# Last FFN of a fused attention and FFN layer: the fourth token group of the batch before it goes behind the transposes of its input, with rounded passes ahead of remainders

## What is computed

```python
def _L0_ffn_ref(x, ln_gamma, ln_beta, fc1_q, fc1_scales, fc1_bias, fc2_q, fc2_scales, fc2_bias):
    ...
    h = (x - mu) * jax.lax.rsqrt(var + EPS) * ln_gamma + ln_beta
    hf = h.reshape(-1, H)
    w1 = _dequant(fc1_q, fc1_scales, G)
    y = hf @ w1 + fc1_bias
    y = jax.nn.silu(y)
    w2 = _dequant(fc2_q, fc2_scales, G)
    z = y @ w2 + fc2_bias
    return residual + 0.5 * z.reshape(residual.shape)
x = L0_attn_x
x = x + _L0_attn_ref(_layernorm(x, axis=-1), L0_attn_Wq, L0_attn_bq, L0_attn_Wk, ...)
x = x + _L0_ffn_ref(_layernorm(x, axis=-1), L0_ffn_ln_gamma, L0_ffn_ln_beta, ...)
```

## Time and profile before

| | us |
|---|---|
| median of 3 runs | 1546.86 |
| lowest, highest | 1544.33, 1548.13 |
| profiled execution, its time | 1547.17 |
| profiled execution, its span | 1545.3 |

### The profile page before, as it was taken

The page is one execution under the profiler, slowest core; times in us unless marked ns, Lnnn a source line. Parts: engine busy times, 40 slices in busy tenths (PEclk is TensorE's granted clock), DMA queues, the critical chain, the costliest instruction groups (busy, mean ns, idle before and its releaser), DMA issues.

```text
span 1545.3 us, 40671 instructions
## 1 busy us (share of the span) xinstructions
PE 1500.6 (97%) x14820; PEld 1307.8 (85%) x14820; DVE 1285.4 (83%) x2587; ACT 1131.0 (73%) x1917; POOL 671.1 (43%) x466
## 2 busy tenths in 40 slices
PE   5799999999999999999999999999999999999997
PEld 5588888888888888888888888888888888888887
DVE  6888888888888888888888888888888888888865
ACT  4487777787777787777787777787777787777763
POOL 3245344544344544344544344544344444344443
PEclk8899999999999999999999999999999999999999
DMA  7946775555775555775556775556775556765540
GB/s 197 218 104 130 176 175 134 138 126 133 176 176 124 140 131 135 176 176 123 123 145 138 176 163 139 132 130 141 176 166 129 127 138 146 176 173 124 112 97 28
DMA packets 153944, 222.96 MB, mean 144 GB/s; under 512 B 20032, under 2 KB 71488, under 8 KB 153920
## 3 DMA queue, kind: packets, MB, share of 16 engines
q1 hardware_dynamic: 152560, 222.63, 60.6%
q10 hardware_dynamic: 1360, 0.01, 0.1%
HBM read 138.69 MB, written 83.89 MB: 144 GB/s over the span
## 4 chain that ended last, share of the span: by engine, by line
PE 89%; DVE 6%; issue 3%; DMA 1%; ACT 0%; SPq 0%; DVEq 0%; POOL 0%; ACTq 0%
PE ring L328 35%; PE ring L390 7%; PE ring L391 7%; PE num L496 6%; PE sc L454 6%; PE sc L328 5%; PE num L463 3%; PE num L328 3%; PE state_acc L328 3%; PE ring L528 2%; PE state_acc L477 2%; PE state_acc L454 1%; DVE xt_lo L654 1%; DVE qk L743 1%; DVE probs L624 1%
## 5 line engine op out<-in xcount | busy, mean ns | idle before, releaser
L1028 POOL TENSOR_TENSOR s_lo<-silu_f,s_hi 128x512 fp32r<-128x512 f32 x256 | 342.9, 1345 | 498.3 <-ACT s_hi L900 498.2
L624 DVE TENSOR_TENSOR probs<-sc,causal 128x512 f32<-128x512 f32 x416 | 271.5, 685 | 71.8 <-PE sc L454 62.0
L328 PE MATMUL ring<-w_hi,s_hi 128*128 128x256 f32 x992 | 282.7, 285 | 1.8 <-issue 1.8
L328 PE MATMUL ring<-w_lo,s_hi 128*128 128x256 f32 x992 | 279.4, 282 | 0.0
L328 PE MATMUL ring<-w_hi,s_lo 128*128 128x256 f32 x992 | 279.3, 282 | 0.0
L328 PEld LDWEIGHTS ring<-w_hi,s_hi 128*128 128x128 f32 x992 | 187.9, 189 | 15.7 <-issue 14.4
L1044 POOL TENSOR_TENSOR qk<-qk,phi_q 128x512 f32<-128x512 f32 x64 | 82.9, 1296 | 262.6 <-DVE qk L677 262.6
L328 PEld LDWEIGHTS ring<-w_lo,s_hi 128*128 128x128 f32 x992 | 188.2, 190 | 1.3
L328 PEld LDWEIGHTS ring<-w_hi,s_lo 128*128 128x128 f32 x992 | 188.0, 190 | 0.0
L390 PE MATMUL ring<-gt_hi,w_q 128*128 128x512 f32 x441 | 187.4, 425 | 0.0
L889 ACT ACTIVATE silu_f<-ring,bias,scale 128x512 f32<-128x512 f32 x217 | 167.4, 771 | 14.1 <-PE ring L391 11.5
(11 more groups left out here) (189 smaller groups left out, 3816.2 us busy)
## 6 DMA issues: line engine op xcount, KB each, us to landing
k_stack<-k_rows SPq DMA_DIRECT2D x192, 256.0 KB, 4.0
q_stack<-q_rows SPq DMA_DIRECT2D x384, 128.0 KB, 6.3
k_rows<-silu_f SPq DMA_DIRECT2D x128, 256.0 KB, 3.8
q_rows<-probs SPq DMA_DIRECT2D x128, 256.0 KB, 4.1
x_in<-in_x SPq DMA_DIRECT2D x32, 512.0 KB, 8.6
xb<-in_x SPq DMA_DIRECT2D x32, 512.0 KB, 8.3
out<-clip SPq DMA_DIRECT2D x64, 256.0 KB, 7.8
silu_f<-in_q SPq DMA_DIRECT2D x2, 512.0 KB, 10.7
```

The source lines that it names most:

```text
L328: last = e.matmul(target, a, b, start=(n == 0), stop=(n == 3 * len(pairs) - 1))
L624: masked[r].done(e.tensor_tensor(half_probs(u, r), score_bank(u, r)[:, :].rearrange("p (h q) -> p h q", h=HV), causal[:, None, :].to_broad ...
L1028: sl.done(e.tensor_tensor(s_lo[:, j, :], silu_f[:, j % SLOTS, :], s_hi[:, j, :].bitcast(F32), ALU.subtract))
```

## The change

Six edits, all of which bear on passes 31 and 32 only (`not A` means pass 32, `not N` passes 31 and 32):

1. The last token group of batch 30, fc2(3), is made in pass 32, behind the transposes of ffn_in and ahead of fc1(0), and its final(1) stands in pass 32 behind gt_lo on DVE.
2. fc2 without N waits for s_hi and s_lo of one feature group at a time.
3. fc2_group makes its eight products with s_hi first and waits for s_lo only ahead of the last four.
4. fc1 waits for gt_lo by half, and TAIL's first pair is swapped, so that the first product of fc1(0) goes to num1.
5. The residual of batch 31 is made behind ffn_sum(2) and no longer ahead of the first ffn_scaled.
6. POOL adds the bias to it by token group, two behind remainder 4 and two behind remainder 5.

```diff
-        TAIL = ((num[0], num[1]), (state_acc, ring[0]), (ring[1], ring[2]))
+        TAIL = ((num[1], num[0]), (state_acc, ring[0]), (ring[1], ring[2]))
...
-                w.need(ht_l, -1)
                 cols = slice(j * P, (j + 1) * P)
                 for t in range(T):
-                    if A or j == 0:
+                    w.need(ht_l, -1, t)
+                    if not A and j == 0:
+                        w.need(attn, -1, 1)
+                    elif A:
                         free_bank(w, f"f{j}{'ab'[t]}", present)
...
-            def fc2(c):
+            def fc2(c, shift=-1):
 
                 if not Fn:
                     return
-                w.need(sh, -1)
-                w.need(sl, -1)
                 n, h = divmod(c, 2)
                 if h == 0:
                     free_bank(w, f"z{n}", present)
+
+                def slices(j):
+                    w.need(sh, shift, j if not N else FT - 1)
+                    w.need(sl, shift, j if not N else FT - 1)
+
                 toks = slice(c * P, (c + 1) * P)
                 last = pe_split3(e, ring_bank(f"z{n}")[:, h * D:(h + 1) * D], [
-                    ((s_hi[:, j, toks], s_lo[:, j, toks]), (w2_hi[:, j, :], w2_lo[:, j, :])) for j in range(FT)])
+                    ((s_hi[:, j, toks], s_lo[:, j, toks]), (w2_hi[:, j, :], w2_lo[:, j, :])) for j in range(FT)], slices)
...
             def fc2_group(j):
 
                 w.need(sh, -1, j)
-                w.need(sl, -1, j)
...
                 for c in range(C):
-                    n, h = divmod(c, 2)
                     toks = slice(c * P, (c + 1) * P)
-                    z = z_bank(n, A)[:, h * D:(h + 1) * D]
-                    e.matmul(z, s_hi[:, j, toks], w2_hi[:, j, :], start=(j == 0 and h == 0), stop=False,
+                    e.matmul(target(c), s_hi[:, j, toks], w2_hi[:, j, :], start=(j == 0 and c % 2 == 0), stop=False,
                              skip_group_check=True)
-                    e.matmul(z, s_hi[:, j, toks], w2_lo[:, j, :], start=False, stop=False, skip_group_check=True)
-                    last = e.matmul(z, s_lo[:, j, toks], w2_hi[:, j, :], start=False, stop=(j == FT - 1),
-                                    skip_group_check=True)
-                    if j == FT - 1 and h:
+                    e.matmul(target(c), s_hi[:, j, toks], w2_lo[:, j, :], start=False, stop=False, skip_group_check=True)
+                w.need(sl, -1, j)
+                for c in range(C):
+                    last = e.matmul(target(c), s_lo[:, j, c * P:(c + 1) * P], w2_hi[:, j, :], start=False,
+                                    stop=(j == FT - 1), skip_group_check=True)
+                    if j == FT - 1 and c % 2:
                         z_pe.done(last)
...
+            if not A:
+                fc2(3, -2)
             fc1(0)
             fc1(1)
...
-            fc2(3)
+            if N:
+                fc2(3)
...
             if Fn and not A:
-                residual()
+                final(1, -2, z_bank(1, True))
...
             ffn_sum(2)
+            if not A and Fn:
+                residual()
...
-            if Fn:
+            if Fn and (N or not A):
                 final(1)
...
                 ffn_lo(j)
-            if Fn:
+                if Fn and not A and j in (4, 5):
+                    w.need(res_m, -1)
+                    for c in (2 * j - 8, 2 * j - 7):
+                        last = e.tensor_tensor(res[:, c, :], res[:, c, :], bias_2[:, :], ALU.add)
+                    if j == 5:
+                        e_res.done(last)
+            if Fn and A:
                 w.need(res_m, -1)
                 e_res.done(e.tensor_tensor(res[:, :, :], res[:, :, :], bias_2[:, None, :].to_broadcast([P, C, D]), ALU.add))
```

More of the change, by code:

```diff
@@ L414, in fc2_group, with target @@
                         w.need(masked[r], -1)
+                def target(c):
+                    return z_bank(c // 2, A)[:, c % 2 * D:(c % 2 + 1) * D]
                 for c in range(C):
-                    n, h = divmod(c, 2)
                     toks = slice(c * P, (c + 1) * P)
-                    z = z_bank(n, A)[:, h * D:(h + 1) * D]
-                    e.matmul(z, s_hi[:, j, toks], w2_hi[:, j, :], start=(j == 0 and h == 0), stop=False,
+                    e.matmul(target(c), s_hi[:, j, toks], w2_hi[:, j, :], start=(j == 0 and c % 2 == 0), stop=False,
                              skip_group_check=True)
-                    e.matmul(z, s_hi[:, j, toks], w2_lo[:, j, :], start=False, stop=False, skip_group_check=True)
-                    last = e.matmul(z, s_lo[:, j, toks], w2_hi[:, j, :], start=False, stop=(j == FT - 1),
-                                    skip_group_check=True)
-                    if j == FT - 1 and h:
+                    e.matmul(target(c), s_hi[:, j, toks], w2_lo[:, j, :], start=False, stop=False, skip_group_check=True)
[4 more added lines that the diff above has]
+                    if j == FT - 1 and c % 2:
                         z_pe.done(last)
@@ L743, in attention, with final @@
                 attn.done(e.tensor_tensor(qk[:, t, :], num[t][:, :], qk[:, t, :], ALU.mult))
[L745 to L749, removed]
+            def final(n, shift=-1, bank_=None):
+                w.need(z_pe, shift, n)
+                w.need(e_res, shift)
+                w.need(store, shift - 1)
                 cs = slice(2 * n, 2 * n + 2)
                 e_out.done(e.scalar_tensor_tensor(
-                    out=clip[:, n, :], in0=z_bank(n, A)[:, :], scalar=0.5,
+                    out=clip[:, n, :], in0=(bank_ or z_bank(n, A))[:, :], scalar=0.5,
                     in1=res[:, cs, :].rearrange("p c d -> p (c d)"), op0=ALU.mult, op1=ALU.add))
```

## The result

| | before | changed |
|---|---|---|
| median of 10 runs, us | 1544.24 | 1540.99 |
| lowest, highest | 1541.9, 1548.13 | 1539.42, 1542.99 |
| profiled execution, span | 1545.3 | 1538.7 |

The ratio of the changed kernel to the one before is 0.9973, 95% interval 0.9964 to 0.9982: 4.2 us faster, 2.8 to 5.6 (the two medians lie 3.25 us apart). The time lies in the forecast range (1538.8 to 1544.2) and near the forecast value (1541.4). That nearness is in part luck: the forecast was counted down from 1546.86 us, the median of three runs, and the median of ten runs of the same kernel is 1544.24; 5.5 us less than that is 1538.7, just outside the range. So the gain is what tells. It is smaller than the 5.5 us of the sum, and it is put together otherwise: the first term was too small, the second too large.

The account below looks back on a forecast made before the run. TensorE, 89% of the chain, was taken as the bound, so only its idle or slow time in the last two passes could be won: 2.5 + 3.0 = 5.5 us off 1546.86 gives 1541.4 us, range 1538.8 to 1544.2.

Parts of the forecast that it names:

- the first term: Pass 31, earlier start of fc2(0) and the clock behind it: 2.5 us gained.
- the second: Everything from the start of fc2(0) and its clock to the last output: 3.0 us gained.
- fc2(0) waits by group: Pass 31: fc2(0) starts when from_state ends, at about 1497.3, and 1.75 us of TensorE idle time go.
- The clock: First token group of fc2 in pass 31, at half clock: removing the pause gains 0.9 to 4.1 us in all, 2.5 taken.
- rival A: The clock never falls in pass 31: 4.1 + 3.0 = 7.1 us gained, 1539.8 us; chance 0.18.
- fc2(3) behind the transposes: Pass 32: ACT's gt_hi starts 1.7 us earlier, fc1(0) at 1518.0 for 1518.76; 0.75 us stay on TensorE.
- Rounded passes ahead of remainders: Last batch's fc2 group 0 starts its s_hi products at 1522.0 and ends at 1523.65 instead of 1525.75: 2.1 us.
- The residual: Moved behind ffn_sum(2) on DVE, 1.37 us, ends at 1525.1; operation for fc1(4) 0.9 us late, which is hidden.
- C: POOL becomes the bound: each 256-column bias addition costs 1.27 us; 3.15 us gained in all, 1543.7 us; chance 0.08.
- D: New TensorE pause at the last transposes lets the clock fall: 2.75 of 5.5 us lost, 1544.1 us; chance 0.10.
- B: Pass 31: the clock comes back at the same instant; 0.9 + 3.0 = 3.9 us gained, 1543.0 us; chance 0.14.
- E: Moved register instruction holds up fc1(0) in each of 29 loop passes: 5.2 us slower, 1552.0 us; chance 0.05.

Follow-up runs that it names:

- b_waits: Kernel before plus only the edit that fc2 without a next batch waits group by group: ratio to the kernel before 0.9978, 3.4 us faster.
- b_fill: Kernel before plus eight extra 512-column products ahead of fc2(0) in pass 31, filling the pause: ratio to the kernel before 0.9990, 1.5 us faster.
- u_waits: Changed kernel with fc2(0) of pass 31 waiting again for all of s_hi and s_lo: ratio to the kernel before 0.9992.
- u_move: Changed kernel with fc2(3) and final(1) of batch 30 back ahead of the transposes: second x1 operation to last two final operations 32.30 us (changed 32.28).
- u_bias: Changed kernel with the bias added once, behind all eight remainders: second x1 operation to last two final operations 32.79 us (changed 32.28).

## Why the prediction was right, and where it was not

*fc2(0) waits by group:* right. The 1.84 us went and nothing took their place.

*The clock:* the mechanism was right, the term was mis-sized. I took 2.5 us of 0.9 to 4.1. The profile gave 4.56 us, rival A, 0.46 us above its own bound; b_waits gave 3.4 us by time (2.0 to 4.8). The step that failed was to call most of the cause "earlier": b_fill and u_waits show that the clock does not fall without the pause. In the eleven profiles in which PE is busy there the clock stayed at 1.00; in the two with the pause it fell. Also, the 6.8 us at half speed in the earlier trace rows were one execution; u_waits had 3.4 us, with PE busy for all of it, so the 5.5 us of busy time after which the forecast let the clock rise are no constant. They were misread in the earlier trace rows too: there the clock was at 0.50 over 70 to 75.5 us as well, with PE busy for 3.17 us of them, and 5.5 us was only the last busy part. A sum made on one profile takes the luck of that execution with it.

*fc2(3) behind the transposes:* its places came as worked out. Counted from the second x1 operation, ACT's gt_hi was 1.58 us earlier (1.7 forecast), fc1(0) 0.77 us (0.75), the first silu_f 1.12 us (1.05). But u_move, with the first silu_f at 11.25 us for 11.26, shows that the last of these came from the residual's leaving, not from the move.

*Rounded passes ahead of remainders:* group 0 ended 2.0 us earlier (2.1 forecast): fc1(4) starts 16.18 us behind the x1 operation, 18.22 us before.

*The residual:* this step failed. "The residual ends at 1525.1" took 1.37 us from a place where POOL was idle and carried it to a place where POOL was not. It took 3.32 us, the operation for fc1(4) came 19.48 us behind the x1 operation, which is later than before (18.89 us), and remainder 3 22.35 us behind it (21.78 before). On DVE and POOL all that had been gained was lost there, and 0.6 us more. PE, 2.0 us ahead at fc1(4), waited for the late s_hi and remainder of group 3 and was only 1.0 us ahead at fc1(7) (24.27 us behind the x1 operation, 25.28 before). POOL then ran without rest to its last remainder, so that group 6 waited too, and 1.5 us were left at the end. I checked what the moved step held up, not what it ran beside.

*The bias:* 0.74 us an addition (0.72 forecast), and the wait for remainder 6 was 0.93 us (0.9):

```profile
1532.73 0.74 PE L430 MATMUL sc<-w_hi,s_lo 128*128 128x256 f32 x4 [0.93 <-POOL s_lo L1041]
```

Taking the late addition off the end was right: the last addition now ends at 1531.46 (1530.02 + 1.44), 3.2 us ahead of the last two operations, and u_bias, which has it at the end again, is 0.51 us longer. C falls.

*Rivals.* D falls: no profile shows a clock below 1.00 at the transposes. B falls as well. E falls: the 27 loop passes between two markers (batches 1 and 28) took 1251.0 to 1253.3 us in the ten profiles with the moved register instruction and 1252.9 to 1254.1 us in the three without; nothing got longer.

The total, 4.2 us by the ratio for 5.5, is right in sign and near in size because two errors of opposite sign met: about +1 us (3.4 for 2.5) and -1.5 us. The absolute time came out nearer still by the luck of the starting value. The gain of 0.27% lies below the bound of 0.3% that the forecast gave 0.63 to pass; its interval (0.18 to 0.36%) reaches over it.

## What to carry to other kernels

A short pause of the matrix engine can cost more than its own length, where what follows it runs at the half clock; here even filling it with useless products paid. Not every pause does this: read the granted clock behind it. When an operation is moved, look also at what the other engines do at the new place: the residual, which DVE makes from one SBUF tile into another, took 2.4 times as long beside GpSimd's remainders (3.32 for 1.37 us). A second edit on the same path may look worthless until the first obstacle behind it is gone, so measure edits again after each repair.

## What was not expected of the hardware

Two of the four residual operations of 0.4 us took 1.38 and 1.37 us beside GpSimd's remainders of 1.3 to 1.4 us, while those nearly kept their length (2.73 us for the two, 2.68 us before). Eight more products on PE made the kernel 1.5 us faster (0.3 to 2.9). The clock's low stretch at the same pause was 6.8 us long in one execution and 3.4 us in another.
